# Another merge of two lists of steps in a two-block transformer kernel

## The reference

```python
x   # (8, 256, 128): 8 sequences of 256 tokens;  ctx_512: (8, 256, 64)
x = x + L0_xattn(layernorm(x), ctx)   # 16 heads of width 8: causal self-attention plus attention over ctx
x = x + L0_ffn(layernorm(x))          # 8 experts 128 -> 512 -> 128, each token weighs its best 2
x = x + L1_xattn(layernorm(x), ctx, ctx)   # one head of width 128: q,k,v; softmax(q k^T) v
x = x + L1_ffn(layernorm(x))          # 16 heads of width 64, values mixed from 8 experts by sigmoid gates
                                      # (top 2), output through the 2 chosen of 8 projections
```

## Time and profile before

| | |
|---|---|
| three runs | 1323.44, 1322.62, 1314.83 us |
| median | 1322.62 us |
| the profiled execution | 1322.67 us, its span of instructions 1320.9 us |
| mean granted TensorE clock | 0.847 of full speed |
| busy share of the span | PE 86%, PEld 67%, DVE 53%, ACT 37%, POOL 6% |

### The profile page before, as it was taken

The page is one execution under the profiler, slowest core; times in us unless marked ns, Lnnn a source line. Parts: engine busy times, 40 slices in busy tenths (PEclk is TensorE's granted clock), DMA queues, the critical chain, the costliest instruction groups (busy, mean ns, idle before and its releaser), DMA issues.

```text
span 1320.9 us, 21222 instructions
## 1 busy us (share of the span) xinstructions
PE 1137.6 (86%) x8499; PEld 883.2 (67%) x8499; DVE 706.6 (53%) x1867; ACT 494.1 (37%) x1022; POOL 85.0 (6%) x134
## 2 busy tenths in 40 slices
PE   6888779989989988989988988988998998985696
PEld 4547545777668765877577855976577766874475
DVE  5514466646565557547665658546664656423500
ACT  4233415352534425451634334442535253422120
POOL 0010002000110002000200011000200011000000
PEclk8558959899789979998889978998889978977556
DMA  7000000242020420142022221042023210133222
GB/s 212 0 1 4 3 0 1 48 69 65 8 49 17 69 55 21 29 76 57 6 49 47 47 47 46 5 77 63 1 48 67 64 40 13 29 56 84 52 44 52
DMA packets 198032, 56.85 MB, mean 43 GB/s; under 512 B 173568, under 2 KB 193838, under 8 KB 197934
## 3 DMA queue, kind: packets, MB, share of 16 engines
q1 hardware_dynamic: 195630, 51.20, 19.9%
q10 hardware_dynamic: 2304, 4.29, 1.1%
HBM read 31.36 MB, written 24.12 MB: 42 GB/s over the span
## 4 chain that ended last, share of the span: by engine, by line
PE 75%; DVE 11%; ACT 7%; issue 3%; SPq 3%; DMA 2%; ACTq 0%; DVEq 0%
PE bank L928 10%; PE bank L737 10%; PE bank L773 9%; PE bank L884 5%; PE bank L663 5%; PE bank L843 4%; PE bank L624 3%; PE bank L678 3%; PE bank L588 3%; DVE negmax L1261 3%; ACT pa L1022 3%; PE bank L942 2%; PE bank L860 2%; PE bank L688 2%; PE bank L911 2%
## 5 line engine op out<-in xcount | busy, mean ns | idle before, releaser
L1022 ACT ACTIVATE pa<-bank 128x512 f32<-128x512 f32 x224 | 123.4, 596 | 122.8 <-PE bank L678 75.8
L1261 DVE TENSOR_REDUCE negmax<-bank 128x2 f32<-128x512 f32 (+1 forms) x224 | 139.0, 683 | 41.9 <-PE bank L526 22.1
L1039 ACT ACTIVATE pa<-bank,b_c 128x256 f32<-128x256 f32 x256 | 107.5, 471 | 128.6 <-PE bank L737 127.3
L928 PE MATMUL bank<-vb,pb 128*128 128x65 f32 x1024 | 137.1, 299 | 4.2 <-issue 4.2
L928 PEld LDWEIGHTS bank<-vb,pb 128*128 128x128 f32 x1024 | 132.8, 214 | 10.3 <-issue 7.9
L737 PE MATMUL bank<-xnT_a,w 128*128 128x256 f32 x512 | 138.1, 417 | 0.1
L773 PE MATMUL bank<-w,pa 128*128 128x128 f32 x1024 | 124.2, 276 | 0.0
L773 PEld LDWEIGHTS bank<-w,pa 128*128 128x128 f32 x1024 | 121.9, 192 | 3.2
L1101 ACT ACTIVATE pb<-bank 128x512 f32<-128x512 f32 x128 | 69.9, 602 | 125.4 <-PE bank L888 125.4
L737 PEld LDWEIGHTS bank<-xnT_a,w 128*128 128x128 f32 x512 | 101.1, 208 | 17.3 <-ACT pa L1039 0.5
L1415 DVE TENSOR_REDUCE negc<-bank 128x2 f32<-128x512 f32 x128 | 80.0, 684 | 58.8 <-PE bank L860 58.6
(11 more groups left out here) (240 smaller groups left out, 1706.3 us busy)
## 6 DMA issues: line engine op xcount, KB each, us to landing
v_d<-at SPq DMA_DIRECT2D x32, 256.0 KB, 3.3
vb<-v_d SPq DMA_DIRECT2D x32, 256.0 KB, 6.0
at_d<-at SPq DMA_DIRECT2D x32, 256.0 KB, 2.1
at<-at_d SPq DMA_DIRECT2D x32, 256.0 KB, 4.4
pv_d<-pvs SPq DMA_DIRECT2D x8, 512.0 KB, 3.1
pvs<-pv_d SPq DMA_DIRECT2D x16, 256.0 KB, 4.2
w<-in_L_ffn_W_dram ACTq DMA_DIRECT2D x1, 2048.0 KB, 11.5
bd<-mix_d SPq DMA_DIRECT2D x128, 8.0 KB
```

Of the source, the lines that this page charges most:

```text
L928: mm = pe.matmul(BB[2 + qt][:, i * (DH + 1):(i + 1) * (DH + 1)], pb[:, h % NPB, kt * T + qt * P:kt * T + (qt + 1) * P], vb[:, kt, h, :], s ...
L1022: nc.scalar.activation(pa[:, e % NPA, :], BA[e % 2][:, :], ACT.Exp, scale=SC0).then_inc(S["a_ex"], 1)
L1039: ins = nc.scalar.activation(hT[:, u % 4, c, :], BA[u % 2][:, c * T:(c + 1) * T], ACT.Relu, bias=b1_c[:, k:k + 1])
L1261: nc.vector.tensor_reduce(negmax[:, i:i + ng], BA[j][:, :].rearrange("p (g k) -> p g k", g=ng), AX, ALU.max, negate=True).then_inc(S["a_mx ...
```

## The change

The same steps are merged in another order. No step is added, removed or altered, and no wait. f_load moves from the scores into the experts, f_norm from a_expert(2) to behind a_expert(6), c_norm_apply and c_q in front of most of the f_stack steps, which now stand singly between the steps of the single-head attention. In stream B b_top2 closes up, b_norm goes before b_out of the sequence ahead, b_max moves forward among the experts, b_mix(0) before b_score(0). The last sequence has new places too.

```diff
--- before.py
+++ after.py
@@ -351,32 +351,31 @@
         def run(name, first, end):
             return [(name, i) for i in range(first, end)]
 
-        STEPS_A = [("a_values", 0), *run("a_max", 0, 7), ("a_shift", 0), ("a_score", 0), ("a_score", 1),
-                   ("f_load", 0), *run("a_score", 2, 14), ("a_lastpv", 0), ("a_heads", 0), ("a_project", 0),
-                   ("c_kv", 0), ("a_norm2", 0), ("a_norm2_apply", 0), ("a_router", 0), *run("a_expert", 0, 3),
-                   ("f_norm", 0), *run("a_expert", 3, 8), ("f_norm_apply", 0), ("a_last", 0), ("c_norm", 0),
-                   *run("f_stack", 0, 4), ("c_norm_apply", 0), ("c_q", 0), ("f_stack", 4), ("c_max", 0),
-                   ("f_stack", 5), ("f_stack", 6), ("c_turn", 0), ("c_out", 0), ("f_stack", 7)]
-        STEPS_B = [("b_norm", 0), ("b_norm_apply", 0), ("b_gates", 0), ("b_top2", 0),
-                   ("b_split", 0), ("b_split", 1), ("b_top2", 1), *run("b_split", 2, 5), ("b_top2", 2),
-                   *run("b_split", 5, 8), *run("b_max", 0, 8), ("b_shift", 0), ("b_score", 0), ("b_fill", 0),
-                   ("b_mix", 0), ("b_mix", 1), ("b_score", 1), ("b_sel", 0), ("b_score", 2), ("b_score", 3),
-                   ("b_attend", 0), ("b_score", 4), ("b_score", 5), ("b_attend", 1),
+        STEPS_A = [("a_values", 0), *run("a_max", 0, 7), ("a_shift", 0), *run("a_score", 0, 14), ("a_lastpv", 0),
+                   ("a_heads", 0), ("a_project", 0), ("a_norm2", 0), ("c_kv", 0), ("a_norm2_apply", 0),
+                   ("a_router", 0), ("a_expert", 0), ("a_expert", 1), ("f_load", 0), *run("a_expert", 2, 7),
+                   ("f_norm", 0), ("a_expert", 7), ("a_last", 0), ("f_norm_apply", 0), ("c_norm", 0),
+                   ("c_norm_apply", 0), ("f_stack", 0), ("c_q", 0), *run("f_stack", 1, 4), ("c_max", 0),
+                   ("f_stack", 4), ("c_turn", 0), ("f_stack", 5), ("c_out", 0), ("f_stack", 6), ("f_stack", 7)]
+        STEPS_B = [("b_norm", 0), ("b_norm_apply", 0), ("b_gates", 0), ("b_top2", 0), ("b_split", 0),
+                   ("b_top2", 1), ("b_top2", 2), *run("b_split", 1, 8), *run("b_max", 0, 8), ("b_shift", 0),
+                   ("b_fill", 0), ("b_mix", 0), ("b_score", 0), ("b_mix", 1), ("b_score", 1), ("b_sel", 0),
+                   ("b_score", 2), ("b_score", 3), ("b_attend", 0), ("b_score", 4), ("b_score", 5),
+                   ("b_attend", 1), ("b_score", 6), ("b_score", 7), ("b_attend", 2), ("b_attend", 3),
+                   ("b_weigh", 0), ("b_gather", 0), ("b_gather", 1), ("b_out", 0)]
+        AFTER_A = (64, 67, 68, 69, 71, 73, 74, 74, 75, 77, 78, 78, 78, 80, 84, 84, 85, 86, 86, 87, 88, 92, 94, 94,
+                   96, 96, 98, 101, 101, 103, 105, 105, 108, 112, 113, 114, 114, 115, 116, 119, 119, 119, 120)
+        assert len(AFTER_A) == len(STEPS_B)
+
+        LAST_B = [("b_norm", 0), ("b_norm_apply", 0), ("b_gates", 0), ("b_top2", 0), ("b_split", 0), ("b_top2", 1),
+                   ("b_split", 1), ("b_top2", 2), *run("b_split", 2, 8), *run("b_max", 0, 4), ("b_fill", 0),
+                   ("b_sel", 0), ("b_mix", 0), ("b_mix", 1), *run("b_max", 4, 8), ("b_shift", 0),
+                   *run("b_score", 0, 4), ("b_attend", 0), ("b_score", 4), ("b_score", 5), ("b_attend", 1),
                    ("b_score", 6), ("b_score", 7), ("b_attend", 2), ("b_attend", 3), ("b_weigh", 0),
                    ("b_gather", 0), ("b_gather", 1), ("b_out", 0)]
-        AFTER_A = (65, 69, 70, 71, 71, 72, 75, 75, 76, 77, 78, 79, 79, 81, 85, 86, 86, 90, 91, 91, 92, 92, 93, 96,
-                   96, 96, 102, 103, 105, 106, 109, 109, 109, 112, 113, 114, 114, 115, 116, 116, 119, 119, 120)
-        assert len(AFTER_A) == len(STEPS_B)
-
-        LAST_B = [("b_norm", 0), ("b_norm_apply", 0), ("b_gates", 0), ("b_top2", 0), ("b_split", 0), ("b_top2", 1),
-                   *run("b_split", 1, 5), ("b_top2", 2), *run("b_split", 5, 8), ("b_max", 0), ("b_fill", 0),
-                   *run("b_max", 1, 4), ("b_mix", 0), ("b_sel", 0), ("b_mix", 1), *run("b_max", 4, 8),
-                   ("b_shift", 0), *run("b_score", 0, 4), ("b_attend", 0), ("b_score", 4), ("b_score", 5),
-                   ("b_attend", 1), ("b_score", 6), ("b_score", 7), ("b_attend", 2), ("b_attend", 3),
-                   ("b_gather", 0), ("b_weigh", 0), ("b_gather", 1), ("b_out", 0)]
-        LAST_AFTER = (57, 66, 75, 76, 76, 76, 76, 76, 76, 76, 76, 89, 104, 109, 109, 109, 109, 109, 110, 110, 110,
-                   110, 117, 117, 117, 117, 117, 117, 117, 117, 117, 117, 118, 126, 129, 136, 136, 143, 147, 149,
-                   149, 154, 154)
+        LAST_AFTER = (64, 66, 66, 66, 66, 71, 71, 71, 72, 72, 79, 79, 79, 79, 79, 79, 79, 79, 79, 79, 79, 80, 82,
+                   95, 105, 115, 116, 129, 132, 148, 156, 157, 157, 157, 157, 157, 157, 157, 159, 159, 159, 159,
+                   159)
         assert len(LAST_AFTER) == len(LAST_B)
 
         def stream_b(q):
```

## The result

The changed kernel takes 1332.58 us (median of 12 runs, 1329.61 to 1343.22), the kernel before 1322.59 (12 runs beside them). The ratio, worked out from all the runs, is 1.0108, with a 95% interval of 1.0081 to 1.0134: 1.1% slower. The two medians alone give 1.0076. The profiled execution took 1334.71 us, its span 1333.0, against a span of 1320.9 before.

A forecast was written before the change was run, and what follows sets the result against it. It took the order of work on PE, with its waits and half-clock stretches, as the bound. From 1322.67 us, +20.4 - 11.9 + 1.4 - 1.0 - 0.5 = +8.4 gave 1331 us, range 1303 to 1349 (the forecast's own 1322 to 1340).

The forecast's parts named there:

- 3.4 us longer: Last expert to the next a_values: 33.4 us instead of 30.0, six times, 20.4 us in all.
- 2.7 forecast: In front of b_attend(0): PE waits 2.7 us in one piece for vb.
- 4.6 forecast: From b_attend(0) on: slow clock behind the wait costs 4.6 us per sequence, chosen from one episode beside the last sequence.
- The sum of 28.8 us at full clock: Last expert to a_values: 28.8 us against 30.0, 1.2 us less, if the clock stays up.
- 1.7 us less per sequence: Scores of stream A: 1.7 us less, bounds 0.5 and 2.5, seven times, 11.9 us in all.
- the slow clock then falls on b_gates and not on a_score(4): Within the scores: slow clock hits b_gates instead of a_score(4) with its products, giving about 1.5 us in every other sequence.
- The experts and a_router, "0.2 us": Later f_load and f_norm, b_max(1) ahead of a_router: cost 0.2 us per sequence, 1.4 over seven.
- c_norm_apply by 4.6, before PE asks for it: Last stretch: c_norm_apply done 4.6 us after the last expert, before PE asks at 5.4 and before POOL clears bd.
- DVE's block is covered: Scores: b_top2(1) and b_top2(2), 7.0 us on DVE, covered by some 10 us before b_split(5); otherwise at most 2.7 us.
- The first sequence and the tail: First sequence 1.0 us less; beside the last sequence 0.5 us less; tail zero, 1 us more at worst.
- the clock stays up: Faster rival: clock does not fall in the wait before b_attend(0); 19 us less, 1303 us; chance 0.2.
- The rival with the slow clock for a whole episode: Slower rival, from b_attend(0) on: slow clock lasts 13.7 us, costing 5.8 each; 1347 us, decides from about 11 us; chance 0.25.

The follow-up runs named there:

- e3: Changed kernel with b_attend(0) moved behind f_stack(5) (in the last sequence behind c_turn); 1295.93 us, ratio 0.9789 to the kernel before.
- e4: Changed kernel with five unread matmuls added before b_attend(0)'s wait for vb, in all sequences but the last; 1306.48 us, ratio 0.9880 to the kernel before.
- e5: Kernel before with only the stretch from a_shift to b_split(7) (the scores) in the new order; 1326.83 us against 1323.97, ratio 1.0018.
- e8: Kernel before with the new order of the last stretch, and b_attend(0) moved behind f_stack(5) there; 1283.74 us, ratio 0.9699.
- e1: Kernel before with only the stretch from the last expert to a_values in the new order; 1320.62 us against 1322.47, ratio 0.9986.
- e6: Kernel before with only the stretch from a_project to a_expert(7) in the new order (b_max(1) ahead of a_router, f_load and f_norm later); 1330.5 us, ratio 1.0051.
- e9: e8 with b_max(1) put ahead of a_router and nothing else; 1296.27 us, ratio 0.9811 to the kernel before.
- e7: Kernel before with only the new places of stream B of the last sequence; 1323.7 us, ratio 1.0000.
- e2: Changed kernel with the stretch from the last expert to a_values back in its old order; 1330.1 us, ratio 1.0062 to the kernel before.
- e12: e8 with five unread matmuls added before a_norm2_apply's wait for the normed tile; 1271.72 us, ratio 0.9605 to the kernel before.
- e11: Kernel before with the new last stretch and b_attend(0) only one step later, behind f_stack(4); 1314.85 us, ratio 0.9951.
- e10: e8 with the scores in the new order too, f_load staying among them; 1294.29 us, ratio 0.9785 to the kernel before.

## Why the prediction was right in its number and wrong in its parts

1331 us was forecast and 1332.6 measured. That the number came out is luck: the last stretch was forecast 5.0 us too dear, the scores 10.0 us too cheap. That leaves 5.0 us, of which the other rows of the table take back 1.4, and the median lies 2.1 below the profiled execution.

- **The last stretch, "3.4 us longer".** Right in kind, as e3 and e4 show: the old waits go, a wait for vb of 2.8 us takes their place (2.7 forecast), and the clock falls in it. The size was 2.6. The price of the slow clock was close: from the start of b_attend(0) to a_values are 14.5 to 15.0 us in the changed kernel and 10.1 in e4's five, 4.4 to 4.9 against 4.6 forecast. The forecast took it from one episode beside the last sequence, and the range of 3.4 to 5.8 that it had shows that 4.6 was a choice in the middle. What was too small is the gain of the order itself. The sum of 28.8 us at full clock is 27.9 in e4, since the steps behind b_attend(0) overlap more than I let them, and b_attend(0) could begin 0.3 us sooner.
- **The scores, "1.7 us less per sequence".** This step failed: it was 0.3 us per sequence, and the same bounds as in the prediction give 36.3 us, not 35. The kernel with the new scores alone (e5) is 0.04 to 0.32% slower. Two parts of it were wrong. The waits of 0.78 and 0.34 us before a_score(13) and a_lastpv did go, but b_split(0) and b_split(4) had covered a_score(6) and a_score(12), and without them 0.78, 0.47 and 0.4 us (in a_score(5), where 0.2 was forecast) are new. I had followed what the moved steps would cover, and not what they left bare. And "the slow clock then falls on b_gates and not on a_score(4)" took its place and length as given: 1.5 us in every other sequence is what a sequence with 10.2 us of it loses to one with 6.8, and the prediction moved the slow time without shortening it. What did shorten was its length, to 6.8 us in most sequences, which the prediction did not have. The new order costs something by itself: with equally much, 6.8 us, at the same place, from some 3.4 us behind the start of a_score(0), the scores take 37.3 to 37.4 us in the new order (e5, and the window of the changed kernel above, clock 0.91) and 36.56 in the old (e8, clock 0.91). The place counts too: two us later the same 6.8 us make the old order take 37.3 to 37.5, in four sequences of e1. As an estimate from these rows: up to 8 us less from the slow time and 0.8 us more per sequence, some 6 in sum, from the order, which leaves about the 1.9 measured.
- **"The experts and a_router, 0.2 us" each.** b_max(1) cost 0.41 at its place, 2.9 over seven, and in the changed kernel nothing was won back behind it (the experts take 0.2 us more; in e6 they gave back 1.3 of 3.0). e6 and e9 show that this was the dearest of the small moves, 6.5 and 12.5 us in the median, though e6 moves more than b_max(1).
- **"c_norm_apply by 4.6, before PE asks for it", "DVE's block is covered"**: right, PE has no wait for either in the timeline. DVE ended c_norm_apply 4.25 us behind the last expert, and PE came to it at 5.4.
- **The first sequence and the tail**: -0.3 and -2.9 instead of -1.0 and -0.5; e7 says that the new places of the last sequence are worth nothing by themselves; where the 2.9 come from stays open.
- **The rival "the clock stays up".** It did not: behind waits of 2.7 to 3.0 us the clock fell six times in six. The rule of the Trainium skill, "TensorE: Matmul & The Clock Gate", section on HAM oscillation, by which only longer gaps would do it, does not hold in these traces. The rival with the slow clock for a whole episode had a slow stretch of 13.7 us; it was 10.2, below the 11 from which it would have decided.

By the ratios the parts alone give -0.14% (e1), +0.18% (e5), +0.51% (e6) and 0.00 (e7), together +0.55, and the whole +1.08 (0.81 to 1.34). By the medians the whole is +0.76 and the parts again +0.55. So a quarter to a half of the loss belongs to no part, and it sits in the last stretch: on top of e2 that costs 0.46% by the ratios (0.2 by the medians), and in e1 it earns 0.14%. In e1's profile the clock fell later in b_attend(0) three times in six, in the changed kernel's at once or nearly so each time. Why it sets in later there stays open; no run moves the clock alone.

## What to carry to other kernels

Price a wait of PE together with the slow clock that may follow it: here 2.8 us of waiting cost 4.4 to 4.9 more. Moving work into this wait (e3) and filling it (e4) each gave back more than the whole change had lost. Where a wait for a transfer can't be shortened, move steps into it that have their inputs (e3, e8), and where there are none, matmuls whose result nobody reads (e4, e12). When a step is moved, list what it covered at its old place before counting what it covers at the new one. And compare the granted clock and the slow time of two traces first: where they differ, terms of a few tenths per sequence don't add up.

## What the runs showed of the hardware

- Useless work made the program faster: 70 matmuls more, 2.0% less time (e4); 80 more, 0.9% less (e12 against e8).
- The wait in front of b_attend(0) behind which the clock falls has no sharp length in these traces: 2.7 to 3.2 us did it each time (changed kernel, e1), 1.8 to 2.0 in two of six (e11), 1.01 and 0.88 twice (e5), a remainder of 0.81 once (e4), and the other remainders of e4, 0.29 to 0.77, not. Behind the waits of 2 us and less the fall came 2.0 to 2.7 us after b_attend(0) had begun; in three sequences of e1, behind 2.9 to 3.2 us, it came 1.8 to 2.0 us after.
- A move of 0.4 us of work changed the slow clock's pattern over the whole period, up to the scores some 100 us on, and cost 12.5 us in sum (e9).
- The same program, e10, ran in 1282.9 to 1297.3 us with clocks of 0.857 to 0.844, while e8, whose sequences all have the same slow stretches, ran within 1.7 us.
- Two operations of DVE, 128x128 from SBUF to SBUF (c_norm_apply), last 2.05 us beside POOL's clearing of bd in all six middle sequences of the kernel before, and 0.60 in all of the changed kernel, where POOL is idle at that time.
